# Four of ten units of attention probabilities turned by DMA instead of by TensorE

## What is computed

```python
latents = x @ W_down.T
keys    = latents @ W_uk.T
values  = latents @ W_uv.T
q = (x @ W_q.T).reshape(b, s, h, dh).transpose(0, 2, 1, 3)
scores = jnp.einsum('bhqd,bhkd->bhqk', q, k) / jnp.sqrt(jnp.float32(dh))
scores = jnp.where(causal, scores, -jnp.inf)
attn = jax.nn.softmax(scores, axis=-1)
ctx = jnp.einsum('bhqk,bhkd->bhqd', attn, v)
return ctx.transpose(0, 2, 1, 3).reshape(b, s, h * dh) @ W_o.T
```

## Time and profile before

| | us |
|---|---|
| median of 3 runs | 256.53 (254.99 to 256.55) |
| the profiled execution: device time | 254.78 |
| its span on the core | 252.8 |
| PE / DVE / ACT / POOL busy | 236.8 / 207.9 / 163.4 / 72.7 |

### The profile page before, as it was taken

One profiled execution on the slowest core, in us unless ns is written; L12 is line 12 of the kernel. 1 busy time (PEld: TensorE's weight loads), 2 busy tenths in 40 slices (PEclk: granted clock), 3 DMA queues, 4 the chain that ended last, 5 costly groups with the idle time before them and its releaser, 6 DMA issues.

```text
span 252.8 us, 7275 instructions
## 1 busy us (share of the span) xinstructions
PE 236.8 (94%) x2643; PEld 181.8 (72%) x2668; DVE 207.9 (82%) x487; ACT 163.4 (65%) x320; POOL 72.7 (29%) x127
## 2 busy tenths in 40 slices
PE   6699998999789999999999999999998899999985
PEld 2555467966667878888788787787887788854464
DVE  2978799996879999989999999999999528368793
ACT  2745580395878888878889798888889400344650
POOL 8320244000002535434344425344355000300310
PEclk9999999999999999999999999999999999999999
DMA  6999300001102103316034150251417220000004
GB/s 221 246 311 352 68 4 0 3 0 42 44 0 54 35 18 87 63 42 125 1 82 83 42 121 3 72 96 32 104 30 86 38 48 3 0 0 3 0 1 166
DMA packets 34792, 17.21 MB, mean 68 GB/s; under 512 B 25484, under 2 KB 34520, under 8 KB 34520
## 3 DMA queue, kind: packets, MB, share of 16 engines
q1 hardware_dynamic: 33576, 15.81, 26.9%
q10 hardware_dynamic: 1200, 1.18, 1.4%
HBM read 7.55 MB, written 1.05 MB: 34 GB/s over the span
## 4 chain that ended last, share of the span: by engine, by line
PE 75%; DVE 14%; DMA 3%; ACT 3%; issue 3%; SPq 1%; DVEq 0%
PE bank L1076 12%; PE bank L877 12%; PE bank L849 9%; PE bank L1151 8%; PE bank L1067 7%; PE bank L1066 4%; PE bank L1090 3%; PE bank L1089 3%; DMA cT<-in_L_ffn_w_dram 3%; PE bank L984 3%; PE bank L1091 3%; PE bank L1023 3%; PE bank L1068 2%; DVE pT_lo L753 2%; DVE nmax L748 2%
## 5 line engine op out<-in xcount | busy, mean ns | idle before, releaser
L503 ACT ACTIVATE prob<-bank,nmax 128x384 f32<-128x384 f32 (+3 forms) x128 | 62.3, 528 | 8.2 <-DVE nmax L744 6.8
L753 DVE TENSOR_TENSOR pT_lo<-bank,pT_hi 128x512 f16<-128x512 f32 x80 | 54.5, 683 | 3.1 <-ACT pT_hi L509 2.4
L509 ACT CAST pT_hi<-bank 128x512 f16<-128x512 f32 x80 | 46.8, 585 | 11.1 <-PE bank L1076 10.7
L1076 PE MATMUL bank<-ident,prob 128*128 128x128 f32 x320 | 50.5, 280 | 0.2 <-ACT prob L503 0.2
L385 POOL TENSOR_TENSOR cst<-craw,rsum 128x256 f32<-128x256 f32 x30 | 18.4, 614 | 94.9 <-DVE craw L762 94.9
L1089 PE MATMUL bank<-lat,pT_hi 128*128 128x65 bf16 x320 | 37.7, 193 | 2.3 <-DVE pT_lo L753 2.3
L1090 PE MATMUL bank<-lat,pT_hi 128*128 128x64 bf16 x320 | 37.8, 195 | 0.0
L1067 PE MATMUL bank<-latT_lo,wqo 128*128 128x384 bf16 (+3 forms) x128 | 36.6, 299 | 1.2
L1091 PE MATMUL bank<-lat,pT_lo 128*128 128x65 bf16 x320 | 37.5, 192 | 0.0
L1089 PEld LDWEIGHTS bank<-lat,pT_hi 128*128 128x128 f16 x320 | 30.1, 96 | 7.2 <-DVE pT_lo L753 2.0
L744 DVE TENSOR_REDUCE nmax<-bank 128x1 f32<-128x512 f32 (+1 forms) x48 | 32.7, 681 | 2.1 <-PE bank L1068 2.1
(11 more groups left out here) (173 smaller groups left out, 470.5 us busy)
## 6 DMA issues: line engine op xcount, KB each, us to landing
wqo<-stage SPq DMA_DIRECT2D x64, 64.0 KB, 2.0
wqo<-in_L_attn_W_q_dram SPq DMA_DIRECT2D x1, 2048.0 KB, 9.7
wqo<-in_L_attn_W_o_dram SPq DMA_DIRECT2D x1, 2048.0 KB, 15.8
out_dram<-X SPq DMA_DIRECT2D x8, 128.0 KB, 1.8
X<-in_L_attn_x_dram ACTq DMA_DIRECT2D x1, 512.0 KB, 6.8
cT<-in_L_attn_W_uk_dram SPq DMA_DIRECT2D x1, 512.0 KB, 11.3
cT<-in_L_attn_W_uv_dram SPq DMA_DIRECT2D x1, 512.0 KB, 11.1
cT<-in_L_ffn_w_dram SPq DMA_DIRECT2D x1, 384.0 KB, 4.9
```

What stands on the lines that cost most here:

```text
L503: last = nc.scalar.activation(prob[:, u % 2, cols], bank[SCORE_BANK[u]][:, cols], ACT.Exp, bias=nmax[:, u, n:n + 1])
L509: nc.scalar.copy(pT_hi[:, j % 2, :], bank[3 + j % 2][:, :]).then_inc(pThi_ready, 1)
L753: nc.vector.tensor_tensor(pT_lo[:, j % 2, :], bank[3 + j % 2][:, :], pT_hi[:, j % 2, :], ALU.subtract).then_inc(pTlo_ready, 1)
L1076: last = nc.tensor.transpose(bank[3 + j % 2][:, blk(k)], prob[:, j % 2, blk(k)], ident[:, :])
```

## The change

- The units 1, 3, 6 and 8 of each pair (`BY_DMA`) are no longer transposed by PE. ACT casts `prob` as it lies (`high_part`), POOL takes the rest (`low_part`), and SP turns both parts, 128 x 1024 values of 16 bits, by one DMA transpose into `turned` (`turn_probabilities`). Two buffers each for the parts and for the turned ones. The other six units (`BY_PE`) go the old way.
- All work ahead of the contexts is moved further ahead (`LEAD` = 7): scores and row_max of unit j+7 in step j (j+4 before), exponent of unit j+6 (j+3 before). The splits stay at j+1 (DVE) and j+2 (ACT). `prob` has 5 buffers (2 before).
- The queries are computed for the pair after the next, in steps 5 and 7; those of pair 1 come ahead of the loop. The first score unit of each pair now uses bank 7, and the first half of the queries waits until that unit's exponent is taken.
- The queries are moved by 4 transfers a pair of twice the width (8 before), and the contexts of a pair by one DMA transpose of twice the width (2 before), except for the last pair.
- The loops now take steps 5 to 14 over six pairs; the rest is written out.

The diff, cut to the orders of work:

```diff
-    SCORE_BANK = [0, 1, 7, 2, 0, 1, 2, 0, 1, 7]
-    HELD_BY = [-3, -2, -1, -4, 0, 1, 3, 4, 5, None]
+    SCORE_BANK = [7, 0, 1, 2, 0, 1, 2, 0, 1, 2]
+    HELD_BY = [None, -3, -2, -1, 1, 2, 3, 4, 5, 6]
+    LEAD = 7
+    BY_DMA = [1, 3, 6, 8]
+    PROBS = 5
...
+            def move_queries(i):
+                sp.wait_ge(u_lo, i * 2 + 2)
+                for side in range(2):
+                    for part in range(2):
+                        sp.dma_start(uc[LAT * part:LAT * (part + 1), i * 2 + side:i * 2 + side + 1, :],
+                                     stage[LAT * side:LAT * (side + 1), part:part + 1, :]).then_inc(u_moved, 16)
+            def turn_probabilities(i, j):
+                d = in_order(BY_DMA, i, j)
+                sp.wait_ge(prob_lo, d + 1)
+                if d >= 2:
+                    sp.wait_ge(turned_used, d - 1)
+                sp.dma_start_transpose(turned[:, d % 2, :, :].rearrange("p a (k q) -> p (a k) q", k=SB),
+                                       prob_hl[:, d % 2, :, :].rearrange("p a n -> p (a n)")).then_inc(prob_turned[d % 2], 16)
...
             for i in range(NP):
+                turn_probabilities(i, 6)
+                turn_probabilities(i, 8)
+                if i > 0:
+                    sp.wait_ge(clo_ready, B + 2 * B * i)
+                    sp.dma_start_transpose(cT[:, i - 1, :, :, :].rearrange("p a n t -> p (a n) t"),
+                                           c_hl[:, i - 1, :, :, :].rearrange("p a n c -> p (a n c)")).then_inc(cT_mid if i == NP - 1 else cT_early, 16)
+                if i < NP - 1:
+                    turn_probabilities(i + 1, 1)
+                if i < NP - 2:
+                    move_queries(i + 2)
+                if i < NP - 1:
+                    turn_probabilities(i + 1, 3)
...
             with pool.Fori(0, NP - 1) as i:
+                low_part(i, 8)
+                divide_context(i, 0, 0)
+                low_part(i, UNITS + 1)
+                divide_context(i, 0, 1)
+                low_part(i, UNITS + 3)
+                divide_context(i, 1, 0)
+                low_part(i, UNITS + 6)
+                divide_context(i, 1, 1)
...
+            def high_part(i, j):          # ACT
+                d = BY_DMA.index(j % UNITS)
+                act.wait_ge(prob_ready, i * UNITS + (j + 1))
+                if not (isinstance(i, int) and i == 0 and j in BY_DMA[:2]):
+                    act.wait_ge(prob_turned[d % 2], i * (8 * ND) + 16 * ((j // UNITS * ND + d) // 2))
+                nc.scalar.copy(prob_hl[:, d % 2, 0, :], prob[:, j % PROBS, :]).then_inc(prob_hi, 1)
             def attention_step(i, j, queries=True):
-                if not beyond(i, j + 3):
-                    exponent(i, j + 3)
-                if queries and j in (1, 3):
-                    split_queries(i + 1, j // 2)
-                if not beyond(i, j + 2):
+                if not beyond(i, j + LEAD - 1):
+                    exponent(i, j + LEAD - 1)
+                    if (j + LEAD - 1) % UNITS in BY_DMA:
+                        high_part(i, j + LEAD - 1)
+                if queries and j in (5, 7):
+                    split_queries(i + 2, (j - 5) // 2)
+                if not beyond(i, j + 2) and (j + 2) % UNITS in BY_PE:
                     split(i, j + 2)
...
             def attention_step(i, j, queries=True):          # DVE
-                if not beyond(i, j + 1):
+                if not beyond(i, j + 1) and (j + 1) % UNITS in BY_PE:
                     split(i, j + 1)
-                if not beyond(i, j + 4):
-                    row_max(i, j + 4)
-                if queries and j in (1, 3):
-                    split_queries(i + 1, j // 2)
+                if not beyond(i, j + LEAD):
+                    row_max(i, j + LEAD)
+                if queries and j in (5, 7):
+                    split_queries(i + 2, (j - 5) // 2)
...
             def queries(i, t):          # PE
+                if not isinstance(i, int) and t == 0:
+                    pe.wait_ge(prob_ready, i * UNITS - UNITS + 1)
...
             def context(i, j):
+                if u in BY_DMA:
+                    pe.wait_ge(prob_turned[d % 2], i * (8 * ND) + 16 * ((j // UNITS * ND + d) // 2 + 1))
+                else:
+                    pe.wait_ge(pTlo_ready, in_order(BY_PE, i, j) + 1)
             def attention_step(i, j, with_queries=True):
-                if with_queries and j in (1, 3):
-                    queries(i + 1, j // 2)
-                if not beyond(i, j + 4):
-                    scores(i, j + 4)
+                if with_queries and j in (5, 7):
+                    queries(i + 2, (j - 5) // 2)
+                if not beyond(i, j + LEAD):
+                    scores(i, j + LEAD)
                 context(i, j)
-                if not beyond(i, j + 2):
+                if not beyond(i, j + 2) and (j + 2) % UNITS in BY_PE:
                     transposes(i, j + 2)
...
+            for t in range(2):
+                queries(1, t)
             pe.wait_ge(lat_lo, 3)
-            for j in range(3):
+            for j in range(LEAD):
                 scores(0, j)
```

More of the change, by code:

```diff
@@ L230, in bass_macaron_moe_mla_moe @@
         u_lo = sem("u_lo")
-        u_moved = [sem(f"u_moved{t}") for t in range(2)]
+        u_moved = sem("u_moved")
         s_ps = sem("s_ps")
@@ L234, in bass_macaron_moe_mla_moe @@
         prob_ready = sem("prob_ready")
+        prob_hi = sem("prob_hi")
+        prob_lo = sem("prob_lo")
+        prob_turned = [sem(f"prob_turned{r}") for r in range(2)]
+        turned_used = sem("turned_used")
         pT_ps = sem("pT_ps")
@@ L293, in _ @@
             sp.wait_ge(woT_hi, 8)
[L294 to L297, removed]
-            for i in range(NP):
[L300 to L308, removed]
@@ L1071, in transposes @@
             def transposes(i, j):
+                n = in_order(BY_PE, i, j)
+                r = BY_PE.index(j % UNITS) % 2
                 pe.wait_ge(prob_ready, i * UNITS + (j + 1))
-                if not (isinstance(i, int) and i == 0 and j < 2):
-                    pe.wait_ge(pTlo_ready, i * UNITS + (j - 1))
+                if not (isinstance(i, int) and n < 2):
+                    pe.wait_ge(pTlo_ready, n - 1)
                 for k in range(SB):
-                    last = nc.tensor.transpose(bank[3 + j % 2][:, blk(k)], prob[:, j % 2, blk(k)], ident[:, :])
+                    last = nc.tensor.transpose(bank[3 + r][:, blk(k)], prob[:, j % PROBS, blk(k)], ident[:, :])
                 last.then_inc(pT_ps, 1)
             def context(i, j):
-                unit = j % HU
+                unit, u = j % HU, j % UNITS
                 if unit == 0 or unit == 2:
                     pe.wait_ge(ctx_free, i * (2 * B) + (j // HU * B + unit // 2 + 1))
-                pe.wait_ge(pTlo_ready, i * UNITS + (j + 1))
+                if u in BY_DMA:
+                    d = BY_DMA.index(u)
+                    pe.wait_ge(prob_turned[d % 2], i * (8 * ND) + 16 * ((j // UNITS * ND + d) // 2 + 1))
+                    parts = [turned[:, d % 2, part, :] for part in range(2)]
+                else:
+                    pe.wait_ge(pTlo_ready, in_order(BY_PE, i, j) + 1)
+                    parts = [p[:, BY_PE.index(u) % 2, :] for p in (pT_hi, pT_lo)]
                 for b, q, at in HEAD_UNITS[unit]:
```

162 lines of the change are left out of this document (102 added, 60 removed).

## The result

| | before | after |
|---|---|---|
| median of the runs, us | 255.76 | 277.92 (276.81 to 279.97) |
| ratio | | 1.088 [1.084, 1.093] |
| the profiled execution: device time, us | 254.78 | 277.99 |
| its span, us | 252.8 | 276.2 |

The changed kernel is slower by 8.8%.

A forecast was written before the change was run, and what follows sets the result against it. The prediction took PE to set the pace before, and in-order waits between ACT and DVE after, at 18.1 us a pair. Last context at 216.8 against 198.4 gave +18.4 on 254.78, 273.2; forecast 274, range 259 to 284.

The forecast's parts named there:

- What it removes: Per pair: PE loses 1.84 us of transposes, DVE 2.4 of splits, ACT nothing in sum, POOL gains 4.6.
- Cover for the DMA: SP's turns and moves take 10.3 us, less than the pair; the tightest, unit 13's, lands at 13.3, wanted 14.5; cost 0.
- The step that decides: Attention loop: ACT and DVE wait for each other in order, so a pair with queries takes 18.1 us instead of 16.2.
- leg: One stretch of work on one engine, handoff included, in the walk from one pair's queries to the next's, 18.12 us in all.
- Ahead of the loop: Start: second pair's queries go first, so the first context starts at 80.3 instead of 72.1; first loop's queries at 87.6.
- The rest: Five more loops of 18.12 to 178.2, then the last pairs; last context ends at 216.8 instead of 198.38: +18.4 us.
- nothing changes: Behind the attention, from the projection on, no time is added, as the earlier contexts are turned well before.
- The signs named for this outcome: Profile after: pairs about 18 us with queries, 16 without, PE some 80% busy, first context near 80, small waits for `turned`.
- PE did not stay the bound: Rival: PE stays the bound, cycle under 14.4 us, -10.7 us, about 245.5 us; chance 0.11.
- the condition that I gave for a gain: In the rival where PE stays the bound: the change gains below a cycle of about 15.9 us.
- The turns were not late: Rival: moves or DMA transposes late, 1.2 to 2.4 us more for each of 6 pairs, 281 to 289 us; chance 0.13.

The follow-up runs named there:

- High parts behind the split: Changed kernel with ACT's high part of unit j+6 placed behind the cast of unit j+2; 264.9 us, ratio 1.034, pair 16.48 us against 18.41.
- cast twice: Changed kernel with each high part cast a first time into a buffer that nobody reads; 295.9 us, ratio 1.152, pair 19.97 us.
- the kernel with all edits of order: Changed kernel with high part and queries behind, start mended, transposes before the context and first split early; 255.5 us, ratio 0.9995 to the kernel before.
- the lead alone: Changed kernel with all ten units transposed by PE, no high or low parts, the rest of the change kept; 267.8 us, ratio 1.046, pair 17.14 us.
- the kernel with the maximum before the split: Changed kernel with DVE taking the maximum of unit j+7 before the split of unit j+1; 267.7 us, ratio 1.045, pair 16.83 us.

## Why the prediction was right, and where it was off

**What it removes.** Right in the amounts: DVE's busy time in a pair fell from 15.43 to 13.16 (2.4 forecast), ACT's stayed at 13.84, POOL's rose by 4.5 (4.6 forecast). None of it bought time.

**Cover for the DMA.** Right, and too careful. By line, the turns and the double transposes on SP (issue ns min/median/max; us to landing):

```profile
L329 SPq DMA_TRANSPOSE turned<-prob_hl x32: 1232/1233/1339, 78.1 to 213.7; - x32
...
DMA to landing us min/median/max: 2.7/2.8/2.9
L341 SPq DMA_TRANSPOSE cT<-wide x7: 1874/2074/2114, 107.4 to 215.0; - x7
...
DMA to landing us min/median/max: 4.3/4.3/4.5
```

A turn lands after 2.8 us (3.3 forecast), the double width costs 2.07 to issue (2.62 estimated), the wide moves 0.60 each as assumed. The cost of 0 for all turns is shown by the kernel without them. The Trainium skill, "VectorE: DVE Perf Modes", section "The three transpose paths", has 1309 ns for one 128x128 block; eight blocks in one transfer land here after 2.8 us. The estimate from its figure was 10.5.

**The step that decides.** This is the part that carried the forecast. Time from the queries' first matmul (126.06) to each leg's end:

| leg ends with | forecast | measured |
|---|---|---|
| cast of 7 starts | 2.87 | 2.90 |
| exponent 13 starts | 4.86 | 4.98 |
| queries' low part starts | 6.93 | 6.99 |
| exponent 16 starts | 10.50 | 10.65 |
| split 12 starts | 12.42 | 12.58 |
| exponent 18 starts | 13.79 | 14.04 |
| split 14 starts | 15.86 | 16.05 |
| exponent 20 starts | 17.23 | 17.44 |
| queries of the next pair start | 18.12 | 18.42 |

The rows of the kernel after at three of these legs, ACT then DVE then PE:

```profile
136.71 0.69 ACT L561 ACTIVATE prob<-bank,nmax 128x512 f32<-128x512 f32 x1 [0.43 <-DVE nmax L818]
137.50 0.62 ACT L570 CAST prob_hl<-prob 128x512 f16<-128x512 f32 x1
138.03 0.58 ACT L576 CAST pT_hi<-bank 128x512 f16<-128x512 f32 x1
...
138.64 0.69 DVE L829 TENSOR_TENSOR pT_lo<-bank,pT_hi 128x512 f16<-128x512 f32 x1 [1.05 <-ACT pT_hi L576]
...
144.48 0.60 PE L929 MATMUL bank<-xT_hi,Mq_hi 128*128 128x512 f16 x2 [1.07 <-ACT prob L561]
```

Every leg is in its place. The 0.3 us missing is one mis-sized term, the handoff: 0.03 was taken for all of them from a single one. From ACT's cast to DVE it holds (138.03 + 0.58 to 138.64). Behind a maximum ACT starts 0.11 to 0.12 later in three of the cycle's four cases (135.91 + 0.68 to 136.71 is one) and 0.04 later in the fourth, exponent 20; why they differ is open, since ACT sat idle before all of them, and before the one that gave 0.03 too. PE starts 0.14 behind the exponent (143.50 + 0.84 to 144.48). ACT's wait for its own result, taken as 0.05, was 0.10 behind exponent 16 (136.71 + 0.69 to 137.50) and 0.03 behind the exponents 13 and 18. High parts behind the split (-1.93) and cast twice (+1.55) show that this cycle was the cause.

**Ahead of the loop.** First context at 81.82, forecast 80.3. The step that failed is the cast and low part that were to end at 69.0: the cast of the second pair's queries needs `stage` free, which SP's moves of the first pair still read. ACT's timeline:

```profile
68.77 0.59 ACT L551 CAST stage<-bank 128x512 bf16<-128x512 f32 x1 [1.52 <-DMA wqo<-stage]
```

**The rest.** The sum was +18.4 us, and the span grew by 23.4. The 5.0 between: 1.6 from the start (first loop's queries at 89.24, forecast 87.6), 5 x 0.3 from the pairs, 0.5 in the last pair (the projection starts at 220.43, where 216.8 was forecast: 3.6 up to here), and 1.4 behind it. There "nothing changes" was wrong in this execution: the granted clock was 0.50 when the projection began. The projection's matmuls started 0.213 us apart until 223.3, and 0.109 later (in the kernel before 0.109 from the first on the earlier trace rows):

```profile
220.43 0.40 PE L1245 MATMUL bank<-Nv_hi,cT 128*128 128x256 bf16 x1
220.62 0.42 PE L1245 MATMUL bank<-Nv_lo,cT 128*128 128x256 bf16 x1
...
223.56 0.27 PE L1245 MATMUL bank<-Nv_lo,cT 128*128 128x256 bf16 x1
```

These errors in the sum all have the same sign; none made up for another. In one place the arithmetic itself slipped: 273.2 with 1.75 added for the median is 275, not 274.

The signs named for this outcome came: pairs of 18.4 us, 15.8 without queries, PE busy for 82% of a pair (15.08 of 18.40), the first context at 81.8, and no wait for `turned` by PE or ACT worth naming.

**The rivals.** PE did not stay the bound; but the condition that I gave for a gain, a cycle below 15.9 us, was about right: at 15.69 the kernel with all edits of order stands level with before, having to pay for a first context at 80 us in place of 72. The turns were not late. What I had not listed is that the lead alone costs: with no turn at all the same order takes 17.1 us a pair.

## What to carry to other kernels

Work taken off the busiest engine is worth nothing where in-order queues of two other engines already wait for each other hand to hand; before such a change, walk one period of the pipeline from instruction to instruction, each queue in its order, and take the longest closed walk, not the largest busy time. When a stage is moved ahead, ask for each engine what now stands between a product and its consumer: here the place of the high parts' casts in one queue was worth 1.93 us a pair, as much as the 16 transposes taken off PE (1.84). A new wait that closes such a walk (a bank freed by the last link) adds an engine's load to another's steps even where both fit side by side: so at least the walk reads in the kernel with the lead alone.

## What the runs showed of the hardware

- Behind the last steps of the attention TensorE's granted clock fell to 0.50, its lower level of 1.2 GHz, from 220 to 222 us, and 0.68 to 224. In the two stretches of 2 us before, PE was busy for 0.88 and 0.96 us. With these waits filled it stayed at 1.00; but it did so too in the kernel with the maximum before the split, unfilled and with the same 0.88 and 0.96 us, and in the kernel with all edits of order, with PE busy for 2.3 of the last 4 us before 198. So PE's busy time in these 4 us does not decide it alone, and what does is not settled. A matmul of 256 columns of the projection takes 0.213 us from start to start at 0.50 and 0.109 at 1.00.
- A DMA transpose of 128 x 2048 values issued by SP takes 2.07 us to issue and 4.3 to land, where two of 128 x 1024 took 1.31 each to issue and 3.3 to land: the cost of one grows less than its size.
- DVE starts 0.03 us behind the cast of ACT that it waited for, even after 1.05 us of idle time, ACT 0.03 to 0.05 or 0.11 to 0.12 behind a maximum of DVE, and PE 0.14 behind an exponent of ACT.
